# Four fused layers on one core: GpSimd's small work of each attention step moved or dropped, and the product with the values put ahead of the reciprocals' transposes

## The reference

```python
# L0: a 32 x 32 matrix per sequence, chosen by an index, mixes the tokens
y = einsum('bct,bcd->bdt', x, w0[conditions])
# L1: attention with a paged cache; q, k, v of 32 tokens x (8, 4, 4) heads x 32, rms and rope on q and k
k_blocks = k_blocks.at[blk, :, off, :].set(k); v_blocks = ...            # new rows written to the cache
scores = einsum('bghtd,bgsd->bghts', qg, k_all) * SCALE
allowed = (kpos <= pos) & (kpos > pos - 128)                             # window of 128
p = softmax(where(allowed, scores, -inf)); o = einsum('bghts,bgsd->bghtd', p, v_all) @ Wo
# L2: base product plus a low-rank adapter per sequence
out = x @ W_base.T + scaling * (((x @ Wt.T) @ A[idx].T) @ B_w[idx].T) @ Wp.T
# L3: again a 32 x 32 matrix per sequence, one of 8
y = einsum('bct,bcd->bdt', x, w3[subjects])
```

## Time and profile before

| what | value |
| --- | --- |
| time, median of 3 runs | 305.37 us (302.78 to 307.06) |
| the profiled execution, own time | 302.65 us |
| its span | 300.8 us |
| PE busy | 210.8 us (70%) |
| DVE busy | 209.0 us (69%) |
| POOL busy | 164.2 us (55%) |
| ACT busy | 131.8 us (44%) |
| mean granted TensorE clock | 0.905 |

### The profile page before, as it was taken

One profiled execution on the slowest core, in us unless ns is written; L12 is line 12 of the kernel. 1 busy time (PEld: TensorE's weight loads), 2 busy tenths in 40 slices (PEclk: granted clock), 3 DMA queues, 4 the chain that ended last, 5 costly groups with the idle time before them and its releaser, 6 DMA issues.

```text
span 300.8 us, 7985 instructions
## 1 busy us (share of the span) xinstructions
PE 210.8 (70%) x2402; PEld 155.9 (52%) x2402; DVE 209.0 (69%) x628; ACT 131.8 (44%) x491; POOL 164.2 (55%) x279
## 2 busy tenths in 40 slices
PE   0132599699899993005788876897868879988773
PEld 0112475455555551004667755675657667767641
DVE  0987947888699985204589876784884867878760
ACT  0220015155444553321756664465555744667510
POOL 4456856067555557754266666556656665673120
PEclk9999859799999998555799998997997998999998
DMA  5819995034611000023031434233424343331011
GB/s 151 258 34 209 211 381 112 17 107 136 194 55 46 29 20 35 32 64 97 4 111 55 118 89 129 73 110 93 142 58 113 95 128 74 115 104 58 20 37 35
DMA packets 18319, 29.70 MB, mean 99 GB/s; under 512 B 8189, under 2 KB 13640, under 8 KB 17906
## 3 DMA queue, kind: packets, MB, share of 16 engines
q0 software_dynamic: 7408, 19.04, 22.9%
q1 hardware_dynamic: 8130, 5.22, 6.0%
q10 hardware_dynamic: 2752, 5.08, 5.4%
HBM read 29.43 MB, written 7.34 MB: 122 GB/s over the span
## 4 chain that ended last, share of the span: by engine, by line
issue 28%; POOL 24%; PE 19%; DMA 16%; DVE 4%; POOLq 4%; ACT 3%; SPq 0%; ACTq 0%; DVEq 0%
DMA big<-in_pool,row_now 4%; DMA w0c<-in_w,w_i 4%; PE quad L1119 4%; POOL own L547 4%; PE quad L1171 4%; POOL big L482 3%; POOL work L504 3%; PE bank L1157 3%; POOL big L542 3%; DMA merged<-work,row_now 2%; POOLq L422 2%; POOL merged L517 2%; DMA big<-merged,row_now 2%; POOL w0c L436 2%; DMA con<-in_consts 2%
## 5 line engine op out<-in xcount | busy, mean ns | idle before, releaser
L699 ACT ACTIVATE work<-bank,nmx 128x164 f32<-128x164 f32 x128 | 49.6, 398 | 30.3 <-DVE nmx L981 24.7
L1157 PE MATMUL bank<-kt_rope,big 128*128 128x164 f32 x256 | 46.8, 319 | 0.0
L1157 PEld LDWEIGHTS bank<-kt_rope,big 128*128 128x128 f32 x256 | 43.4, 205 | 5.0 <-issue 0.8
L995 DVE TENSOR_TENSOR onT<-quad,rT 32x256 f32<-32x256 f32 x64 | 26.9, 420 | 21.9 <-PE quad L1171 20.4
L1153 PE MATMUL bank<-mask,identb 128*128 128x492 bf16 (+1 forms) x48 | 18.2, 379 | 30.3 <-DVE kt_rope L972 22.7
L981 DVE TENSOR_REDUCE nmx<-bank 128x3 f32<-128x492 f32 (+1 forms) x48 | 28.5, 593 | 12.3 <-PE bank L1157 12.1
L1119 PE MATMUL quad<-wqkv_sb,work 128*128 128x512 f32 x64 | 34.2, 660 | 2.8 <-ACT work L652 2.7
L988 DVE STREAM_TRANSPOSE work<-work 128x768 f32<-128x768 f32 (+2 forms) x96 | 34.7, 410 | 0.0
L682 ACT ACTIVATE big<-qT,con 128x256 f32<-128x256 f32 (+1 forms) x64 | 27.2, 512 | 0.1
L517 POOL DMA_INDIRECT merged<-work,row_now x16 | 18.3, 1141 | 15.4 <-ACT work L646 9.0
L436 POOL DMA_INDIRECT w0c<-in_w,w_i x16 | 16.9, 1054 | 17.9 <-DMA w0c<-in_w,w_i 7.1
(11 more groups left out here) (158 smaller groups left out, 469.6 us busy)
## 6 DMA issues: line engine op xcount, KB each, us to landing
merged<-big ACTq DMA_DIRECT2D x3, 1024.0 KB
xin<-in_x SPq DMA_DIRECT2D x16, 128.0 KB
out<-x4s SPq DMA_DIRECT2D x16, 128.0 KB, 2.0
w3bd<-in_w SPq DMA_DIRECT2D x64, 4.0 KB
con<-in_consts SPq DMA_DIRECT2D x1, 660.5 KB, 5.2
wqkv_sb<-in_wqkv ACTq DMA_DIRECT2D x1, 512.0 KB
wt_sb<-in_wt ACTq DMA_DIRECT2D x1, 256.0 KB
wp_sb<-in_wp ACTq DMA_DIRECT2D x1, 256.0 KB
```

The source lines that it names most:

```text
L699: act.activation(prob[:, p, hd, 0:NK], ps_sc[(p + i) % 2][:, j * NK:j * NK + NK], ACT.Exp, bias=nmx[:, p, hd:hd + 1], scale=1.0, accum_out ...
L995: ve.tensor_tensor(onT[rows, :, :].rearrange("p c (b n) -> p b c n", b=NB), ps_o[rows, :, 64 * (g % 2):64 * (g % 2) + 64].rearrange("p b ( ...
L1157: mm = pe.matmul(at[:, j * NK:j * NK + NK], qbd[:, p, hd, :], kT[:, p, hd // GSZ, 0:NK], start=False, stop=(j == n - 1), skip_group_check= ...
```

## The change

1. **Reciprocals on DVE.** One DVE reciprocal reads the 8 sums with a broadcast and writes all 256 columns of `rwide`. The 128x8 reciprocal (L1010) and POOL's two copies (L563) go, and the semaphore between them.
2. **The product first.** PE runs `weighted(t1)` ahead of the two transposes of `rwide`. ACT's copy to `rT` moves behind `exponents(1)`.
3. **Masks once.** DVE makes the masks of all 16 tiles in two instructions (128 x 2048 and 128 x 1152) at the beginning of the attention stage; they hold 0 or 1, and `identb` holds the factor -1e30. PE reads them with an address that depends on the step. POOL makes no masks.
4. **w3 plus identity once.** SP loads the 8 matrices, DVE adds the identity (32 x 256), SP stores them to device memory and loads each tile's four from there. POOL's L578 goes. `w3bd` is now read by PE itself, so SP waits for the last layer of tile t - 2 (`l3_done`) where it waited for POOL's addition.
5. **No copies of columns.** `fetch` and `cached` read their row numbers from `idx` itself.
6. **POOL's attention stage unrolled**, with constants in its waits instead of a register.

```diff
...
             sp.dma_start(subj_sb[:, :], subject).then_inc(s_num, 16)
+            sp.dma_start(w3e[:, :, :], w3.rearrange("n c d -> c n d")).then_inc(s_w3e, 16)
...
             sp.wait_ge(s_zero, ZEROED)
+            sp.wait_ge(w3e_done, 1)
+            sp.dma_start(w3_d.rearrange("n c d -> c n d"), w3e[:, :, :]).then_inc(s_w3d, 16)
+            sp.wait_ge(s_w3d, 16)
...
                     if reused(t):
-                        sp.wait_ge(w3i_done, t - 1)
-                    diagonal(t, p, w3, subj_sb, w3bd, s_w3)
+                        sp.wait_ge(l3_done, t - 1)
+                    diagonal(t, p, w3_d, subj_sb, w3bd, s_w3)
                 t, k, p = at_step(h, u, 3)
...
-                pl.tensor_copy(row_now[:, 0, r:r + 1], idx[:, 0, bass.ds(t, 1)]).then_inc(row4_copied, 1)
-                wait(row4_copied, t + 1)
                 pl.indirect_dma_start(
                     out=kvb[:, r, :], out_offset=None, in_=pool_rows4,
-                    in_offset=bass.IndirectOffsetOnAxis(ap=row_now[:, 0, r:r + 1], axis=0),
+                    in_offset=bass.IndirectOffsetOnAxis(ap=idx[:, 0, t:t + 1], axis=0),
                     bounds_check=4 * NPOOL - 1, oob_is_err=False, engine_sem=desc_cache).then_inc(s_cache[r], 16)
                 wait(desc_cache, t + 1)
-
-            def masks(t, p):
-
-                pl.tensor_copy(pos_now[:, :, p:p + 1], pos3[:, 0:2, bass.ds(t, 1)]).then_inc(pos_copied, 1)
-                wait(pos_copied, t + 1)
-                pl.tensor_scalar(mask[:, p, 0:NKB], cc("backpos"), pos_now[:, 0, p:p + 1], NEG,
-                                 ALU.is_lt, ALU.mult).then_inc(mask_done, 1)
-                pl.tensor_scalar(mask[:, p, NKB:NK], cc("ownpos"), pos_now[:, 1, p:p + 1], NEG,
-                                 ALU.is_gt, ALU.mult).then_inc(mask_done, 1)
...
                         wait(s_init, 16 * OWN)
-                    pl.tensor_copy(row_now[:, 3, r:r + 1], idx[:, 3, bass.ds(t, 1)]).then_inc(row1_copied, 1)
+                    pl.tensor_copy(row_now[:, r:r + 1], idx[:, 3, bass.ds(t, 1)]).then_inc(row1_copied, 1)
                     wait(row1_copied, t + 1)
                     wait(v_copied, t + 1)
                     wait(krow_done, t + 1)
                     pl.indirect_dma_start(
-                        out=merged, out_offset=bass.IndirectOffsetOnAxis(ap=row_now[:, 3, r:r + 1], axis=0),
+                        out=merged, out_offset=bass.IndirectOffsetOnAxis(ap=row_now[:, r:r + 1], axis=0),
                         in_=kvrow[:, r, :], in_offset=None,
                         bounds_check=SEGS * BLOCK - 1, oob_is_err=False, engine_sem=desc_scat).then_inc(s_scat[r], 16)
                     wait(desc_scat, t + 1)
                 if isinstance(h, int) and 4 <= 4 * h + u < 4 + RING:
                     cached(4 * h + u - 4, u % RING)
-                if isinstance(h, int) and NT <= 4 * h + u < NT + 2:
-                    masks(4 * h + u - NT, u % 2)
...
-                pl.tensor_copy(row_now[:, 1:3, r:r + 1], idx[:, 1:3, bass.ds(t, 1)]).then_inc(rowm_copied, 1)
-                wait(rowm_copied, t + 1)
                 wait(s_cache[r], 16 * (n + 1))
                 pl.indirect_dma_start(
                     out=kvb[:, r, :], out_offset=None, in_=merged_rows4,
-                    in_offset=bass.IndirectOffsetOnAxis(ap=row_now[:, 1, r:r + 1], axis=0),
+                    in_offset=bass.IndirectOffsetOnAxis(ap=idx[:, 1, t:t + 1], axis=0),
                     bounds_check=SEGS * 4 - 1, oob_is_err=False, engine_sem=desc_fetch).then_inc(s_merge[r], 16)
                 wait(desc_fetch, 2 * t + 1)
                 pl.indirect_dma_start(
                     out=own[:, r, :], out_offset=None, in_=merged_rows2,
-                    in_offset=bass.IndirectOffsetOnAxis(ap=row_now[:, 2, r:r + 1], axis=0),
+                    in_offset=bass.IndirectOffsetOnAxis(ap=idx[:, 2, t:t + 1], axis=0),
                     bounds_check=SEGS * 8 - 1, oob_is_err=False, engine_sem=desc_fetch).then_inc(s_own[r], 16)
                 wait(desc_fetch, 2 * t + 2)
             fetch(0, 0, 0)
             fetch(1, 1, 0)
-            def phase2(h, u):
-                t, k, p, r, n = at_step4(h, u, 1)
-                if valid(t):
-                    wait(rden_done, t + 1)
-                    if not isinstance(t, int) or t >= 1:
-                        wait(rT_done, t)
-                    for c in range(2):
-                        pl.tensor_copy(rwide[:, 128 * c:128 * c + 128].rearrange("p (g d) -> p g d", g=G),
-                                       rden[:, p, :].rearrange("p (g c) -> p c g", c=2)[:, c].unsqueeze(2)
-                                       .broadcast_to([128, G, HD])).then_inc(rwide_done, 1)
-                t, k, p, r, n = at_step4(h, u, 2)
+            for s in range(NT + 2):
+                t = s - 2
                 if valid(t):
                     wait(zs_done, t + 1)
-                    if not isinstance(t, int) or t >= 1:
+                    if t >= 1:
                         wait(l2_done, t)
                     pl.tensor_tensor(zm[0:E * R, :].rearrange("p (b c) -> p b c", b=NB),
                                      zs[:, :].rearrange("p (b c) -> p b c", b=NB),
-                                     zscale[:, bass.ds(t * NB, NB)].unsqueeze(2).broadcast_to([E * R, NB, TOK]),
+                                     zscale[:, t * NB:t * NB + NB].unsqueeze(2).broadcast_to([E * R, NB, TOK]),
                                      ALU.mult).then_inc(zm_done, 1)
-                    wait(s_w3[p], 64 * (k + 1))
-                    if reused(t):
-                        wait(l3_done, t - 1)
-                    pl.tensor_tensor(w3i[:, p, :], w3bd[:, p, :], ident, ALU.add).then_inc(w3i_done, 1)
-                t, k, p, r, n = at_step4(h, u, -1)
-                if valid(t) and reused(t):
-                    wait(sc_done, 3 * (t - 1))
-                    masks(t, p)
-                t, k, p, r, n = at_step4(h, u, -2)
-                if valid(t):
-                    fetch(t, r, n)
-                t, k, p, r, n = at_step4(h, u, -3)
-                if valid(t) and (not isinstance(t, int) or t >= RING):
+                t = s + 2
+                if valid(t):
+                    fetch(t, t % RING, t // RING)
+                t = s + 3
+                if valid(t) and t >= RING:
                     wait(pv_done, t - 3)
-                    cached(t, r)
-
-            steps(pl, phase2, NT + 2, *P2R[1:])
+                    cached(t, t % RING)
...
             act.wait_ge(s_con, 16)
-            act.copy(identb[:, :], ident).then_inc(s_prec, 1)
+            act.activation(identb[:, :], ident, ACT.Copy, scale=NEG).then_inc(s_prec, 1)
...
                     exponents(0)
+                if valid(t):
+                    exponents(1)
                 if valid(t1):
                     act.wait_ge(rT_done, t1 + 1)
                     if not isinstance(t1, int) or t1 >= 1:
                         act.wait_ge(onT_done, G * t1)
                     act.copy(rT[:, :, :], ps_t.rearrange("p (c n) -> p c n", c=2)).then_inc(rT_copied, 1)
-                if valid(t):
-                    exponents(1)
                 tn, _, pn, _, _ = at_step4(h, u, -1)
...
                         op0=ALU.mult, op1=ALU.mult))
+            ve.wait_ge(s_w3e, 16)
+            ve.tensor_tensor(w3e[:, :, :], w3e[:, :, :], cc("ident", TOK)[:, 0:TOK].unsqueeze(1)
+                             .broadcast_to([TOK, 8, TOK]), ALU.add).then_inc(w3e_done, 1)
+
             def same_blocks():
...
+            for k, (name, a, b, op) in enumerate((("backpos", 0, NKB, ALU.is_lt), ("ownpos", NKB, NK, ALU.is_gt))):
+                ve.tensor_tensor(mask[:, :, a:b], cc(name).unsqueeze(1).broadcast_to([128, NT, b - a]),
+                                 pos3[:, k, :].unsqueeze(2).broadcast_to([128, NT, b - a]), op).then_inc(mask_done, 1)
             keys(0, 0, 0, 0)
...
                     ve.wait_ge(exp_done, H * (t1 + 1))
-                    ve.reciprocal(rden[:, p1, :], den[:, p1, :]).then_inc(rden_done, 1)
+                    if not isinstance(t1, int) or t1 >= 1:
+                        ve.wait_ge(rT_done, t1)
+                    ve.reciprocal(rwide[:, :].rearrange("p (c g d) -> p c g d", c=GSZ, g=G),
+                                  den[:, p1, :].rearrange("p (g c) -> p c g", c=GSZ).unsqueeze(3)
+                                  .broadcast_to([128, GSZ, G, HD])).then_inc(rwide_done, 1)
                 if valid(t2):
...
                     pe.wait_ge(qbd_done, NB * (t + 1))
-                    pe.wait_ge(mask_done, 2 * (t + 1))
+                    pe.wait_ge(mask_done, 2)
                 if i == 2:
                     pe.wait_ge(exp_done, H * t + 3)
                 elif not isinstance(t, int) or t >= 1:
                     pe.wait_ge(exp_done, H * t - 2 + 2 * i)
                 n = len(HEADS[i])
                 pe.matmul(at[:, 0:n * NK], identb[:, :],
```

(10 more changed lines are left out.)

17 lines of the change are left out of this document (8 added, 9 removed).

## The result

The changed kernel takes **333.77 us** (median of 4 runs, 332.01 to 335.41), beside 304.11 us for the kernel before on the same chip: 1.096 times as long, 95% interval 1.091 to 1.101. The forecast of 313.0 us, with its range up to 320, had the direction and missed by 21 us.

What follows compares the result with a forecast made beforehand. POOL (9.98 us a step) was taken to bound ten of sixteen steps, DVE right behind. Steps 16r - 14.3 and start -4.0 gave +8.9 with r = 1.7, 311.6, plus half of 2.7: 313.0 us, range 299 to 320.

Steps and rivals of the forecast that it cites:

- The product first: PE's transposes and ACT's copy now stand between product and DVE's scaling: net +0.35 us a step.
- the step of 7.93 us: DVE's step where POOL doesn't hold it up, taken as base: 7.93 + 0.35 + r, 9.98 us with r = 1.7.
- at POOL's pace: Ten of sixteen attention steps, 9.85 us each, taken as held by POOL's 9.98 us a step.
- The total of the rest: Sum over steps, end and start: 16r - 18.3, or +8.9 us with r = 1.7, giving 311.6 us.
- r: What the 256-column DVE reciprocal's occupancy adds to the 128x8 one's 0.08 us: bounded by 0.26 and 2.5, taken as 1.7.
- The reciprocal: The deciding term: DVE's 128x8 reciprocal becomes 256 columns wide ahead of `zs`, adding r = 1.7 us a step.
- r near 2.05: Reciprocal read as eight cycles a column at 0.96 GHz: 2.13 us, a sum 5.6 us above the forecast's.
- The order: PE's product ahead of the transposes in each attention step: +0.35 us a step.
- POOL's floor of 8.8 us: POOL's own round, 5.08 + 1.85 + 1.85, with the cached gather's landing bare: 8.8 against 9.98 us a step.
- The start: Before the first steps: POOL's mask pairs -3.2, column copies -1.1, identity addition +0.35; together -4.0 us.
- SP's later wait: SP waits for the last layer of t - 2 instead of POOL's addition: at least one whole step covers it, costs nothing.

Runs made afterwards that it cites:

- e3: Changed kernel with POOL's two fetches issued only after the product of the same step: 309.26 us, 1.015 of the kernel before.
- e1: Changed kernel with the 128x8 reciprocal back and a DVE copy spreading it to 256 columns: 304.01 us, 0.999 of the kernel before.
- e2: Changed kernel with the transposes ahead of the product again and ACT's copy ahead of its second exponents: 321.79 us, 1.059 of the kernel before.
- e14: Changed kernel with `merged` declared as an output tensor instead of a scratch tensor: 309.83 us, 1.021 of the kernel before.
- e15: Changed kernel with its two fetches from `merged` taking the cached gather's index column, so other rows: 310.16 us, 1.024 of the kernel before.
- e17: Changed kernel with a second scratch tensor of 64 MB declared ahead of `merged`: 310.09 us, 1.023 of the kernel before.
- e18: Changed kernel with the 128x8 reciprocal, a DVE copy spreading it, and `merged` as an output tensor: 289.92 us, 0.959 of the kernel before.
- e11: Changed kernel with narrow reciprocal and DVE copy, fetches after the product, and the cached gather ahead of them: 287.84 us, 0.952 of the kernel before.
- e12: Changed kernel with narrow reciprocal, DVE copy, late fetches, cached gather ahead of them, and transposes ahead of the product again: 288.73 us, 0.954.
- e6: Changed kernel with narrow reciprocal and DVE copy, and fetches after the product, which stays ahead of the transposes: 292.1 us, 0.964 of the kernel before.
- e16: Kernel before with only POOL's cached gather moved ahead of the two fetches: 306.84 us, 1.013 of the kernel before.

## Why the prediction was wrong, and where it was right

**The step that failed is a constant**, in "The product first": the step of 7.93 us, which POOL doesn't hold up, was carried over whole, with the 1.65 us that its product takes, and only the transposes were added to it (+0.35). It comes from a trace in which the fetches hardly ever ran beside the product. The prediction looked at how long POOL's round would be, and not at what its fetches would then stand beside. In the changed kernel `zm` opens POOL's round, waits for `zs`, and so puts both fetches beside the product, which then takes 3.3 us, 12 times. Issued behind the product instead (e3, on the chip of e1 and e2), they leave it at 1.65 us, and the kernel takes 309.26 us, 24 less. That is shown. Why a fetch there stretches the product, and why e14, e15 and e17 are free of it, stays open.

The 24 us come apart in the profiled executions of the changed kernel and e17, 332.01 and 310.37 us. From the first weights to the last they differ by 21.2 us: a stalled step is 1.5 us longer at full clock, so 18 for twelve, and the other 3 lie in the three steps whose granted clock is lower, two of them of 12.7 us (243.91 and 267.94). An ordinary step and the first of these, then the stretch of 0.50 in it, right behind its product:

```profile
232.52:243.91 11.39, 8.20 (x132) 6.38 (x131) 8.63 (x20) 5.53 (x22) 3.42 (x4) 1.00 0.33 91
243.91:256.57 12.66, 10.35 (x134) 7.76 (x133) 8.64 (x21) 5.62 (x22) 3.42 (x4) 0.87 0.33 100
```
```profile
251.90:254.00 2.10, 2.10 (x9) 1.73 (x9) 0.83 (x2) 1.36 (x4) 0.99 (x1) 0.50 0.18 59
```

One row of the kernel before spoke of the stall, the 2.94 us product at 149.32 with the gather L542 issued at 150.46. Its granted clock was 1.00, so the clock doesn't account for it, and the prediction didn't read it. Four other products there are long too, 2.12 to 2.86 us, but at mean granted clocks of 0.50 to 0.73 (186.08, 205.92, 226.48 and 246.35 us). The first of them:

```profile
186.08:188.95 2.87, 2.87 (x98) 2.54 (x97) 0.00 (x0) 2.68 (x10) 1.71 (x5) 0.50 0.40 151
```

They stand in the four steps of 11.6 to 11.9 us; the other six of the ten "at POOL's pace" take 8.2 to 9.4. The prediction averaged the two kinds to 9.85 us and put all of it down to POOL. What part is the clock's, no run separates.

**The total of the rest holds, in part by luck.** With the measured r = 1.55 it gives 16 x 1.55 - 18.3 = +6.5 us; e14 is 309.83 - 303.38 = +6.5 above its kernel before, e17 310.09 - 302.75 = +7.3. But its terms miss both ways: in e17's profiled execution the first weights come 1.4 us earlier than before where the forecast had 4.0, and the steps and the end cost some 1.5 us less than forecast.

- The reciprocal: 1.63 us of occupancy, r = 1.55 for the 1.7 taken. Narrow against wide without the stall is 309.83 - 289.92 = 20 us (e14, e18), less than 16 x 1.55 = 25; their profiled executions differ by 25.2, so with e18's spread the missing 5 say nothing.
- The Trainium skill's eight passes for a reciprocal (page "VectorE: DVE Perf Modes", section "First, the fixed hardware budget"), read as eight cycles a column, gave an estimate of r near 2.05. The trace has 1.63 / 256 = 6.4 ns a column, 6.1 cycles at that page's 0.96 GHz, so that reading is too dear.
- The order: 9.89 - 7.93 - 1.55 = 0.41 us a step in e17, for 0.35; 0.5 us a step by e2 in the stalled kernel. With a narrow reciprocal it is nothing (e11, e12).
- POOL's floor of 8.8 us: hidden in the changed kernel, as said, and visible in e6. But why it was 9.98 before was half told: e16 shows POOL's own instructions filling 9.78 us of a round, and the longer rounds holding waits for PE at a low clock.
- The start: first keys at 133.56 us for 136.15, first weights at 143.26 for 145.75: -2.5 of the forecast -4.0, and in e17 134.39 and 144.30. The masks on DVE take 2.25 and 0.75 us and are hidden; DVE still waits 9.02 us for the gathers.
- SP's later wait cost nothing that shows in e17's steps.

Against the kernel before, in medians from different chips: relief and start with a narrow reciprocal -13 (e18), the wide reciprocal +20 (e14 over e18), the stall +24 (changed over e14, and over e3): +31, for the +29.7 measured, with a kernel before that differs by 1.4 us between the times. Of the three the stall alone was missing in the forecast.

## What to carry to other kernels

When an edit frees an engine that issues DMAs, work out where in the step its transfers start now, and look in the trace of before for the one step in which they overlap the critical product; an odd long instance at full clock is the warning. A duration is a constant only beside the same neighbours. Where matmuls of a few ns each are stretched without a wait, move the gather behind them first: that is shown here. Before a cause is read from kernels that lack an effect, run the one that has it beside them on the same chip, and look on the page at what they moved. And narrow first, spread later: a reciprocal costs by its output columns (0.08 us for 8, 1.63 for 256 here).
